# Two key tiles per TensorE step, VectorE and GpSimd sums dealt anew, interleaved operand planes, and a bisection turned onto the partitions

## The reference

```
x = x + attn0(layernorm(x))     # 8 heads of 32, softmax over 1024 keys, K and V from a 64-wide latent
x = x + ffn0(layernorm(x))      # 14 experts, top-2 of a softmax router, gelu
x = x + attn1(layernorm(x))     # 16 heads of 8, linear attention with cumulative sums
x = x + ffn1(layernorm(x))      # 8 experts, top-1, at most 1280 tokens each, dropped ones go to expert 0
```

## Time and profile before

| | |
|---|---|
| runs | 2599.93, 2605.22, 4977.18 us |
| the profiled execution | 2597.67 us, span 2595.9 us |
| TensorE (PE) busy | 2020.2 us, 78% of the span |
| VectorE (DVE) busy | 1793.1 us, 69% |
| GpSimd (POOL) busy | 1517.6 us, 58% |
| ScalarE (ACT) busy | 1044.5 us, 40% |
| granted TensorE clock, mean of the span | 0.878 |

### The profile page before, as it was taken

The page is one execution under the profiler, slowest core; times in us unless marked ns, Lnnn a source line. Parts: engine busy times, 40 slices in busy tenths (PEclk is TensorE's granted clock), DMA queues, the critical chain, the costliest instruction groups (busy, mean ns, idle before and its releaser), DMA issues. The chain is left out here.

```text
span 2595.9 us, 49294 instructions
## 1 busy us (share of the span) xinstructions
PE 2020.2 (78%) x12582; PEld 1018.9 (39%) x12582; DVE 1793.1 (69%) x4359; ACT 1044.5 (40%) x1646; POOL 1517.6 (58%) x1114
## 2 busy tenths in 40 slices
PE   7957999999999999999976639947767775210993
PEld 3422333333333333333335538834444443100993
DVE  7845888888888888888848854428888787630222
ACT  4522444444444444444434415523444443010441
POOL 3433666666666666666647753358888873035452
PEclk9877999999999999999986659978999887555996
DMA  6753212211221122112112323310000000011776
GB/s 194 247 174 116 61 55 63 63 59 58 64 62 58 59 64 61 56 62 63 53 49 98 120 88 126 126 55 22 19 19 20 19 17 7 10 40 61 220 225 193
DMA packets 182752, 209.55 MB, mean 81 GB/s; under 512 B 28560, under 2 KB 140688, under 8 KB 182672
## 3 DMA queue, kind: packets, MB, share of 16 engines
q1 hardware_dynamic: 160416, 177.36, 22.0%
q0 software_dynamic: 12800, 26.27, 3.0%
q10 hardware_dynamic: 9456, 5.11, 0.6%
HBM read 128.37 MB, written 80.00 MB: 80 GB/s over the span
## 5 line engine op out<-in xcount | busy, mean ns | idle before, releaser
L592 DVE TENSOR_REDUCE halfmax<-p_m 128x1 f32<-128x512 f32 x1024 | 680.6, 691 | 160.8 <-PE p_m L484 156.7
L584 ACT ACTIVATE probs<-p_s 128x1024 f32<-128x1024 f32 x512 | 522.3, 1023 | 544.9 <-PE p_s L502 544.1
L473 POOL TENSOR_TENSOR sum_p<-sum_p,probs 128x1024 f32<-128x1024 f32 x256 | 604.1, 2360 | 153.8 <-ACT probs L584 138.9
L484 PE MATMUL p_m<-ka,qa 128*128 128x512 bf16 x1024 | 399.3, 390 | 34.3 <-DMA vh<-v 29.9
L501 PE MATMUL p_s<-qa,ka 128*128 128x512 bf16 x1024 | 392.0, 383 | 13.7 <-DMA qb<-max_lo 13.7
L502 PE MATMUL p_s<-qb,kb 66*128 66x512 bf16 x1024 | 391.3, 382 | 0.0
L509 PE MATMUL p_o<-probs,vh 128*32 128x256 f32 x4096 | 327.6, 392 | 14.9 <-ACT probs L584 14.9
L473 POOL TENSOR_TENSOR sum_p<-probs 128x1024 f32<-128x1024 f32 x64 | 151.0, 2359 | 251.9 <-ACT probs L584 251.9
L1462 PE MATMUL ln_p_cum<-ln_kv,c_tri 128*128 128x512 f32 (+1 forms) x384 | 168.1, 581 | 54.8 <-POOL ln_kv L1406 54.7
L484 PEld LDWEIGHTS p_m<-ka,qa 128*128 128x128 bf16 x1024 | 99.4, 97 | 283.1 <-DVE halfmax L592 181.0
L1132 ACT ACTIVATE e_h<-e_p_h,e_w 128x256 f32<-128x256 f32 x316 | 126.1, 473 | 175.8 <-PE e_p_h L1111 175.6
(11 more groups left out here) (266 smaller groups left out, 3139.6 us busy)
## 6 DMA issues: line engine op xcount, KB each, us to landing
e_w<-in_weights SPq DMA_DIRECT2D x40, 514.0 KB
qa<-q SPq DMA_DIRECT2D x128, 128.0 KB
ka<-k SPq DMA_DIRECT2D x128, 128.0 KB
e_xb<-xs SPq DMA_DIRECT2D x78, 128.0 KB
ys<-e_y SPq DMA_DIRECT2D x78, 128.0 KB, 1.9
v<-pj_v SPq DMA_DIRECT2D x8, 1024.0 KB, 5.0
qb<-q SPq DMA_DIRECT2D x128, 64.0 KB
kb<-k SPq DMA_DIRECT2D x128, 64.0 KB
```

The costliest lines, as they stand in the source:

```text
L473: nc.gpsimd.tensor_tensor(sum_p[s % 2][:, :], (sum_p[s % 2] if n else probs[0])[:, :], probs[k][:, :], ALU.add).then_inc(sum_p_d, 1)
L484: nc.tensor.matmul(p_m[n % 2][:, :], qa[s][:, (n // 2) * P:(n // 2 + 1) * P], ka[s][:, (n % 2) * HALF:(n % 2 + 1) * HALF], start=True, sto ...
L584: nc.scalar.activation(probs[k][:, :], p_s[k % 2][:, :], ACT.Exp, scale=SCALE).then_inc(probs_d, 1)
L592: nc.vector.reduce_max(halfmax[:, n % 2, n // 2:n // 2 + 1], p_m[n % 2][:, :], AX.X).then_inc(max_read, 1)
```

## The change

In words: `key_tiles` is the new step of TensorE: the scores of two tiles (8 matmuls) with one maximum half after each pair of them, then the values of two tiles one behind the other. Each of the 16 halves has its place: four per step. The turned maxima come into the same two banks in turn (`max_bank`, `turn_bank`). VectorE reduces the 16 halves in order, and its other work is put between them in pieces: the split after half 1, the reciprocal in two pieces after halves 5 and 7, the product after 9, and its addition in two pieces of 128x512 after halves 11 and 13. It adds tiles 1 and 3 now, GpSimd tiles 0, 2, 4, 5, 6, 7. `load` takes seven DMAs of 64 or 128 partitions, whose sources have the 32 rows of a head as outermost dimension with the planes inside it, and `project` puts k's planes in the order low, high, middle so that neighbouring ones can be fetched together. In `capacity` TensorE turns the probabilities, eight DMAs lay them out with 16 partitions for each expert (128x512), and the bisection keeps one threshold per partition: one comparison that also sums (L1889), a matmul with a matrix of ones within an expert's 16 partitions, and two small operations.

```diff
-                        for s, dram in ((0, q3), (1, k3)):
-                            store(g, part, plane, ready, sent, s, dram)
+                        store(g, part, plane, ready, sent, 0, q3)
+                        store(g, (part + 1) % 3, plane, ready, sent, 1, k3)
...
-MAX_PLAN = (0, 3, 0, 3, 3, 3, 3, 1)
-POOL_SUMS = (1, 2, 4, 5, 6)
+TURN = 2
+POOL_SUMS = (2, 4, 5, 6, 7)
+VECTOR_SUMS = (1, 3)
...
-        LOADS, LAST = 9, UNITS // SLOTS - 1
+        LOADS, LAST = 7, UNITS // SLOTS - 1
...
-            def rows(dram, part):
-                return dram[part, bass.ds(u, 1)].rearrange("o d t -> (o d) t")
-            def parts(dram):
-                return dram[0:2, bass.ds(u, 1)].rearrange("a o d t -> a (o d) t")
+            def parts(dram, which):
+                return dram[which, bass.ds(u, 1)].rearrange("a o d t -> (o d) a t")
             for i in range(2):
-                sp.dma_start(qa[s][i * 64:(i + 1) * 64, :], rows(q3, i).unsqueeze(0).broadcast_to([2, DH0, T])).then_inc(operands_in[s], 16)
-                sp.dma_start(ka[s][i * 64:(i + 1) * 64, :], parts(k3)).then_inc(operands_in[s], 16)
-            for i, (qp, kp) in enumerate(((0, 2), (2, 0))):
-                sp.dma_start(qb[s][i * DH0:(i + 1) * DH0, :], rows(q3, qp)).then_inc(operands_in[s], 16)
-                sp.dma_start(kb[s][i * DH0:(i + 1) * DH0, :], rows(k3, kp)).then_inc(operands_in[s], 16)
+                sp.dma_start(qa[s][i * 64:(i + 1) * 64, :], parts(q3, slice(i, i + 1)).broadcast_to([DH0, 2, T])).then_inc(operands_in[s], 16)
+                sp.dma_start(ka[s][i * 64:(i + 1) * 64, :], parts(k3, slice(1, 3))).then_inc(operands_in[s], 16)
+            sp.dma_start(qb[s][0:2 * DH0, :], parts(q3, slice(0, 3, 2))).then_inc(operands_in[s], 16)
+            sp.dma_start(kb[s][0:2 * DH0, :], parts(k3, slice(0, 2))).then_inc(operands_in[s], 16)
...
+            if n == TURN:
+                pe.wait_ge(max_read, u * 2 * KT + TURN)
+            elif n == TURN + 1 and not first:
                 pe.wait_ge(max_parts, ONE + u)
-            if n >= 2:
+            elif n > TURN or not first:
                 pe.wait_ge(max_read, u * 2 * KT + n - 1)
-            nc.tensor.matmul(p_m[n % 2][:, :], qa[s][:, (n // 2) * P:(n // 2 + 1) * P],
...
-            spread(pe, s, 1, c["ones"][:, 0:DH0], sum_p[s % 2], False, False)
-            spread(pe, s, 1, c["ones"][:, 0:DH0], sum_v[s % 2], False, True).then_inc(den_d, 1)
...
-        def key_tile(pe, r, s, k):
-            halves = list(range(sum(MAX_PLAN[:k]), sum(MAX_PLAN[:k + 1]))) if exists(r, s, 2) else []
-            nxt = (r, s, k + 1) if k + 1 < KT else (*after(r, s), 0)
-            for h in range(2):
-                if exists(*nxt[:2]):
-                    score(pe, *nxt, h)
-                if halves:
-                    max_half(pe, *after(r, s, 2), halves.pop(0))
-            if k == 0 and exists(r, s, 1):
-                max_turn(pe, *after(r, s))
-            values(pe, r, s, k)
-            for n in halves:
-                max_half(pe, *after(r, s, 2), n)
+            pe.wait_ge(sum_v_d, SV0 + 2 * u + 2)
+            spread(pe, s, 1, c["ones"][:, 0:DH0], sum_v[s % 2], False, False)
+            spread(pe, s, 1, c["ones"][:, 0:DH0], sum_p[s % 2], False, True).then_inc(den_d, 1)
+        def key_tiles(pe, r, s, k):
+            n = 2 * k
+            for i in (k + 2, k + 3):
+                nxt = (r, s, i) if i < KT else (*after(r, s), i - KT)
+                for h in range(2):
+                    if exists(*nxt[:2]):
+                        score(pe, *nxt, h)
+                    if n == TURN and exists(r, s, 1):
+                        max_turn(pe, *after(r, s))
+                    if exists(r, s, 2):
+                        max_half(pe, *after(r, s, 2), n)
+                    n += 1
+            for i in (k, k + 1):
+                values(pe, r, s, i)
...
                         else:
                             act.wait_ge(sum_p_d, SP0 + (u - 1) * len(POOL_SUMS) + 1 + (POOL_SUMS.index(k) if k else 0))
...
             u = r * SLOTS + s
-            dve.wait_ge(probs_d, (u + 1) * KT)
-            dve.wait_ge(den_d, DEN0 + u - 1)
-            nc.vector.tensor_tensor(sum_v[s % 2][:, :], probs[3][:, :], probs[7][:, :], ALU.add).then_inc(sum_v_d, 1)
+            cols = slice(half * HALF, (half + 1) * HALF)
+            if half == 0:
+                dve.wait_ge(probs_d, u * KT + max(VECTOR_SUMS) + 1)
+                dve.wait_ge(den_d, DEN0 + u - 1)
+            nc.vector.tensor_tensor(sum_v[s % 2][:, cols], probs[VECTOR_SUMS[0]][:, cols], probs[VECTOR_SUMS[1]][:, cols],
+                                    ALU.add).then_inc(sum_v_d, 1)
+        def invert(dve, r, s, half):
+            u = r * SLOTS + s
+            cols = slice(half * Q // 2, (half + 1) * Q // 2)
+            if half == 0:
+                dve.wait_ge(den_d, DEN0 + u + 1)
+                dve.wait_ge(o_d, O0 + u)
+            nc.vector.reciprocal(inv[:, cols], p_o[s % 2][:, 1, cols]).then_inc(inv_d, 1)
...
+            def segment(r, s, last=None):
+                ahead, coming = after(r, s, 2), after(r, s)
+                if exists(*coming):
+                    row_maxima(dve, *coming)
+                for n in range(2 * KT):
+                    if n == TURN and exists(*coming):
+                        split_maxima(dve, *coming)
+                    if exists(*ahead):
+                        half_max(dve, *ahead, n)
+                    if last is not None and n in (5, 7):
+                        invert(dve, *last, n // 2 - 2)
+                    if last is not None and n == 9:
+                        normalise(dve, *last)
+                    if n in (11, 13):
+                        add_tiles(dve, r, s, n // 2 - 5)
+            for n in range(2 * KT):
...
-            def segment(r, s):
-                if exists(r, s, 2):
-                    half_maxima(dve, *after(r, s, 2), LATE)
-                    row_maxima(dve, *after(r, s, 2))
-                add_last_tiles(dve, r, s)
-                if exists(r, s, 2):
-                    split_maxima(dve, *after(r, s, 2))
-                if exists(r, s, 3):
-                    half_maxima(dve, *after(r, s, 3), EARLY)
-                normalise(dve, r, s)
...
+            mm.then_inc(pturned_d, 1)
+            pe.wait_ge(own_d, OWN)
+            for k in range(BITS):
...
-                    k = r * STEPS + m
-                    nc.vector.tensor_tensor(cmp[:, :, :], p_of[:, :, :], wide(trial[:, :]), ALU.is_ge).then_inc(loop_d, 1)
-                    dve.wait_ge(loop_d, k * 4 + 1)
-                    nc.vector.tensor_reduce(count[:, :], cmp[:, :, :], AX.X, ALU.add).then_inc(counted, 1)
-                    dve.wait_ge(total_d, k + 1)
-                    nc.vector.scalar_tensor_tensor(out=rise[:, :], in0=p_count[:, 0:E1], scalar=float(CAP1), in1=bit[:, :],
-                                                   op0=ALU.is_ge, op1=ALU.mult).then_inc(loop_d, 1)
-                    dve.wait_ge(loop_d, k * 4 + 2)
-                    nc.vector.tensor_tensor(level[:, :], level[:, :], rise[:, :], ALU.add)
-                    nc.vector.tensor_scalar(bit[:, :], bit[:, :], 0.5, None, ALU.mult).then_inc(loop_d, 1)
-                    dve.wait_ge(loop_d, k * 4 + 3)
-                    nc.vector.tensor_tensor(trial[:, :], level[:, :], bit[:, :], ALU.add).then_inc(loop_d, 1)
-                    dve.wait_ge(loop_d, k * 4 + 4)
+            dve.wait_ge(pturned_d, 1)
+            nc.vector.tensor_copy(turned[:, :, :], p_turned[:, :, :]).then_inc(turned_d, 1)
+            step(nc.vector.tensor_tensor(p_of[:, :, :], p_of[:, :, :], equal[:, :, :], ALU.add))
+            apart(dve, probs_in, E1 * 16, passed)
+            for k in range(BITS):
+                bit = 2.0 ** -(k + 1)
+                nc.vector.tensor_scalar(above[:, :], probs[:, :], trial[:, :], None, ALU.is_ge, ALU.add, accum_out=part[:, :]).then_inc(tried, 1)
+                step(nc.vector.tensor_scalar(base[:, :], trial[:, :], -0.5 * bit if k + 1 < BITS else -bit, None, ALU.add))
+                dve.wait_ge(total_d, k + 1)
+                step(nc.vector.tensor_scalar(rise[:, :], p_count[:, 0:1], float(CAP1), bit, ALU.is_ge, ALU.mult))
+                step(nc.vector.tensor_tensor(trial[:, :], base[:, :], rise[:, :], ALU.add))
+            dve.wait_ge(own_d, OWN)
+            nc.vector.tensor_scalar(level[:, :], first_of[:, :], trial[:, :], None, ALU.mult).then_inc(level_d, 1)
+            dve.wait_ge(total_d, BITS + 1)
...
+            for e in range(E1):
+                rows = turned[(e % 2) * TILES:(e % 2 + 1) * TILES, e // 2, :]
+                sp.dma_start(probs[e * SPLIT:(e + 1) * SPLIT, :].rearrange("g (t p) -> g t p", p=P), rows).then_inc(probs_in, 16)
```

(33 more changed lines are left out.)

104 lines of the change are left out of this document (55 added, 49 removed).

## The result

An execution of the changed kernel takes 2643.3 us in the median of four (2639.38 to 2644.8); the ratio to the kernel before is 1.0156, 95% interval 1.0136 to 1.0176. It is that of the fast runs: for the kernel before a fourth run, 2601.28, is among them, and the one of 4977.18 is not. 2653 was forecast, case A.

| | before | after | difference |
|---|---|---|---|
| `project` (SyncE's first load of `attend`) | 167.27 | 170.04 | +2.8 |
| first load to first scores | 53.46 | 29.88 | -23.6 |
| `attend`, 61 units at their mean | 17.39 | 18.67 | +78.1 |
| `attend`, the rest (filling and draining) | | | +2.1 |
| `capacity` | 103.95 | 84.61 | -19.3 |

The account below looks back on a forecast made before the run. TensorE was taken to bind the old kernel; after the change, VectorE's loop through the maximum banks, with additions waiting for GpSimd. Sum: 2597.7 + 98 (units) - 23 (start) - 19 (`capacity`) = 2653 us; range 2580 to 2690, case A's own 2636 to 2670.

Parts of the forecast that it names:

- case A: In `attend`, VectorE's half additions wait out GpSimd's additions: unit 19.0 us, total 2653 us, range 2636 to 2670; chance 0.60.
- The unit: One unit of `attend` lengthens from 17.39 to 19.0 us, +98 us over 61 units (88 to 107).
- The chain through the banks: In `attend`, two banks for the maxima make VectorE wait for halves 2 to 4: 3.9 us a unit.
- VectorE's own work: In `attend`, from the start of reduction 4 to the end of the next unit's reduction 1: 13.05 us, without slack.
- The waits: In `attend`, VectorE's two half additions wait for GpSimd's third and fourth additions: 1.36 and some 0.9 us a unit.
- The start: Start of `attend`: loads on more DMA engines, and the 13.66 us wait for copied maxima goes: -23 us.
- capacity: Bisection in `capacity`: 27 steps of 1.88 instead of 2.83 us, less about 7 for setup and epilogue: -19 us (-12 to -27).
- TensorE's own unit: In `attend`, values in pairs cut TensorE's unit from 17.0 to 16.1 us, if nobody keeps it waiting.
- E: Rival in `attend`: two banks can't bridge a pair of values, VectorE idles in every step; +110 us, about 2762; chance 0.04.
- D: Rival at the start of `attend`: additions wait, but the loads come no sooner; 2675 us; chance 0.06.
- C: Rival in `attend`: only one of the two half additions waits; unit 18.2 us, +49, 2604 us; chance 0.10.
- B: Rival in `attend`: half additions don't wait, falling between GpSimd's or not blocked; unit 17.1 us, 2537 us; chance 0.17.

Follow-up runs that it names:

- oneinput: Changed kernel with each half addition replaced in place by a maximum over 512 columns of one SBUF tile; ratio to the kernel before 0.9628, unit 16.49 us.
- gap: Changed kernel with VectorE's two half additions moved from behind reductions 11 and 13 to behind reduction 3; ratio to the kernel before 0.9617, unit 16.49 us.
- again: The changed kernel itself, no edit, on one of the experiments' chips; ratio to the kernel before 1.0166, unit 18.69 us.
- product: Changed kernel with VectorE's product moved behind the first half addition, from ahead of reductions 10 and 11; ratio to the kernel before 0.9792, unit 17.14 us.

## Why the prediction was right

**The sum.** The forecast adds up to 2653.7, and the profiled execution took 2639.38. The unit was put 20 too high; `project`, the filling and draining of `attend` and the other stages, all put at nothing, brought back 6.5.

**The unit (+98 forecast, +78 measured).** The mechanism is case A's: L623 takes 2.75 and 1.63 (2.66 and 1.67 in the mean of 64), TensorE waits for `halfmax`, and `oneinput` and `gap` show that nothing else of the change makes the unit long. The profile was to show L623 at 1.5 to 2.1 and TensorE idle for 3 us; the first piece is longer than that, and TensorE idles for 2.2. The chain through the banks was forecast at 3.9 from the end of reduction 1 to reduction 4; from the split, which follows reduction 1 at 820.83, it is 824.67 - 820.83 = 3.84, with the idle time of 1.93 in it. Two terms were off, against each other:

- VectorE's own work between reduction 4 and the end of reduction 1 was put at 13.05. It is 14.83 less the waits, 11.8. The duration of 0.66 for a reduction came from three in 1.99; that was the pace of TensorE's three matmuls (3 x 0.218). Queued reductions take 0.57 to 0.63 (1.14 to 1.26 from the start of a pair to what follows).
- The waits were put at 1.36 and 0.9; they are 2.1 and 1.0. VectorE comes at +6.78, not +7.5, and since it is held until GpSimd's third addition ends, whatever it saved before went into the wait. That is why an error of 1.3 in one term became one of 0.3 in the unit. The unit is a loop of its own: 1.77 from reduction 4 to GpSimd (1.8 forecast), 9.97 for four additions, 0.54 to the end of the second piece, four reductions and the row maxima with little overlap (2.55), 3.84.

**The start (-23, measured -23.6; -23.0 alone)** and **`capacity` (-19, measured -19.3)** came as worked out: steps of 1.90 for 1.88, 4.9 more ahead of the first step, where 6 stood, and 0.9 behind the last. Of the 6 the turn with its copy and the landing (2) had no row behind them. In the result the eight issues end at 2268.72, and the first comparison starts 1.55 later.

**`project`** stood at nothing and ends 2.8 later. `again`, which is the same program, and `product` show the same; the other eight runs with the same `project` don't (166.2 to 167.6 instead of 169.8 to 170.1). So it is not the edit of `project`; what it is stays open. **TensorE's own unit** was put at 16.1 and is 16.2 busy with 0.24 of waiting for the turn's bank, in `gap`.

**The rivals.** E has no row: there is no idle time ahead of halves 8 and 12. It is hidden rather than absent: in `gap`, where VectorE comes sooner, it waits 0.78 for half 12 (810.29), which costs nothing there because TensorE is full. D is refuted by the start, C by the two rows of L623. B, that the pieces fall between GpSimd's additions, was given 0.17 and argued against with "none of it lies between reductions 11 and 14". That argument was weaker than it read: the pieces needn't fall into idle time, only come ahead of GpSimd's next addition, and 0.14 us decided that (0.13 or 0.14 in each of 58 units). The forecast had put 0.9 there: VectorE at +7.5, GpSimd's third addition from +6.6; they came at +6.78 and +6.64. `product` is nearly case B (17.14, where 17.1 stood), made by moving one instruction. So the mechanism was right, and that case A came and not B was luck: the error in VectorE's own work took 0.7 of the 0.9 away, and a little more would have turned the result.

## What to carry to other kernels

Where VectorE and GpSimd both read two operands from SBUF, place VectorE's instruction in a stretch in which GpSimd waits for something else, and look there first: here the same two instructions cost 2.2 us a unit in one place and nothing in another. If one must meet GpSimd, what it costs is the rest of GpSimd's instruction, whatever work is saved before it; and put work of the engine that is waited for between two such pieces, never the pieces behind each other. A duration read from a row in which the engine was paced by another is an upper bound of its own.
